# Softplus in the state-space stage: the limit on exp(-|x|) moved from VectorE to ScalarE

## The reference

```python
xz = x @ in_w
u, z = jnp.split(xz, 2, axis=-1)
uc = cb + sum((up[:, k:k + L, :] * cw[:, k] for k in range(D_CONV)))   # up: u, padded
u = jax.nn.silu(uc)
proj = u @ xpw                              # dt | Bm | Cm
delta = jax.nn.softplus(dt @ dtw + dtb)
A = -jnp.exp(A_log)
def step(h, inp):
    d_t, b_t, c_t, u_t = inp
    dA = jnp.exp(d_t[..., None] * A)
    h = dA * h + (d_t * u_t)[..., None] * b_t[:, None, :]
    return (h, jnp.einsum('bdn,bn->bd', h, c_t))
y = (ys + u * Dp) * jax.nn.silu(z)
return y @ ow                               # then x = layer_norm(y + x)
```

## Time and profile before

| | |
|---|---|
| median of 3 timed runs | 3722.86 us |
| the profiled execution | 3724.66 us |
| its span (first to last instruction) | 3722.9 us |
| mean granted TensorE clock | 0.888 of full speed |
| TensorE busy | 2960.9 us, 80% |
| VectorE busy | 2872.0 us, 77% |
| GpSimd busy | 1987.2 us, 53% |
| ScalarE busy | 1850.2 us, 50% |
| scan, 512 instructions | 1170.5 us |
| GpSimd's product with C, 512 instructions | 1212.0 us |

### The profile page before, as it was taken

The page is one execution under the profiler, slowest core; times in us unless marked ns, Lnnn a source line. Parts: engine busy times, 40 slices in busy tenths (PEclk is TensorE's granted clock), DMA queues, the critical chain, the costliest instruction groups (busy, mean ns, idle before and its releaser), DMA issues. The chain is left out here.

```text
span 3722.9 us, 48371 instructions
## 1 busy us (share of the span) xinstructions
PE 2960.9 (80%) x18386; PEld 1614.7 (43%) x18386; DVE 2872.0 (77%) x3833; ACT 1850.2 (50%) x2899; POOL 1987.2 (53%) x1022
## 2 busy tenths in 40 slices
PE   8968899556599378988898889988898889558733
PEld 3447888433477233434343434334343434234412
DVE  3667676756211349999999999999999999987688
ACT  2433343124111057766776677657775677424334
POOL 0024554212300328788888888798878887842100
PEclk8878887678699689999999999999999999888856
DMA  1000000000333323444434343444444444430000
GB/s 49 0 1 4 4 4 3 7 20 0 124 123 126 77 94 134 156 141 155 150 133 149 129 173 134 148 142 143 155 150 137 143 137 145 138 105 12 2 20 23
DMA packets 120561, 343.54 MB, mean 92 GB/s; under 512 B 14875, under 2 KB 45554, under 8 KB 119570
## 3 DMA queue, kind: packets, MB, share of 16 engines
q1 hardware_dynamic: 114450, 331.91, 26.3%
q0 software_dynamic: 3072, 6.00, 0.8%
q10 hardware_dynamic: 2816, 2.62, 0.2%
HBM read 328.21 MB, written 14.68 MB: 92 GB/s over the span
## 5 line engine op out<-in xcount | busy, mean ns | idle before, releaser
L2014 POOL TENSOR_TENSOR mb_h<-mb_h,mb_BC 128x1024 f32<-128x1024 f32 x512 | 1212.0, 2386 | 407.1 <-DVE mb_h L2261 407.1
L2261 DVE TENSOR_TENSOR_SCAN mb_h<-mb_dA,mb_bx 128x1024 f32<-128x1024 f32 x512 | 1170.5, 2286 | 23.8 <-ACT mb_dA L2128 6.0
L2364 PE MATMUL mb_y<-mb_h,ident 128*128 128x512 f32 x2048 | 998.9, 627 | 216.4 <-POOL mb_h L2014 214.3
L2128 ACT ACTIVATE mb_dA<-mb_delta,mb_A 128x511 f32<-128x511 f32 x1024 | 664.9, 713 | 417.2 <-DVE mb_h L2261 412.1
L2364 PEld LDWEIGHTS mb_y<-mb_h,ident 128*128 128x128 f32 x2048 | 386.8, 198 | 792.1 <-issue 415.9
L2257 DVE TENSOR_TENSOR mb_bx<-mb_du,mb_BC 128x1024 f32<-128x1024 f32 x512 | 630.3, 1231 | 41.4 <-DMA mb_BC<-mamba_BC 4.5
L250 PE MATMUL mb_p<-mb_xT,mb_in_w 128*128 128x512 f32 x512 | 237.3, 607 | 23.2 <-ACT mb_sz L2054 16.7
L250 PE MATMUL mb_p<-mb_upad,mb_convd 128*128 128x512 f32 x512 | 225.0, 592 | 0.8 <-ACT mb_upad L2042 0.8
L1738 DVE TENSOR_TENSOR me_h<-me_s,me_p 128x320 f32<-128x320 f32 x64 | 31.2, 488 | 220.4 <-ACT me_s L1715 220.4
L1692 POOL DMA_INDIRECT me_y<-expert_results,slot x32 | 31.1, 971 | 258.4 <-DMA expert_results<-me_oe 248.9
L250 PEld LDWEIGHTS mb_p<-mb_xT,mb_in_w 128*128 128x128 f32 x512 | 98.8, 195 | 152.3 <-issue 117.9
(11 more groups left out here) (438 smaller groups left out, 5401.3 us busy)
## 6 DMA issues: line engine op xcount, KB each, us to landing
mb_BC<-mamba_BC SPq DMA_DIRECT2D x256, 1024.0 KB, 5.2
me_W<-in_L_ffn_W SPq DMA_DIRECT2D x24, 1024.0 KB, 9.4
mb_in_w<-in_L_attn_in_proj_w SPq DMA_DIRECT2D x4, 1024.0 KB, 8.1
mb_convd<-in_mamba_taps SPq DMA_DIRECT2D x4, 1024.0 KB, 10.2
expert_rows<-me_zero SPq DMA_DIRECT2D x1, 2560.0 KB, 10.1
x<-in_x SPq DMA_DIRECT2D x4, 512.0 KB, 6.2
me_xe<-expert_rows SPq DMA_DIRECT2D x8, 256.0 KB, 10.5
expert_results<-me_oe ACTq DMA_DIRECT2D x8, 256.0 KB, 7.5
```

The costliest lines, as they stand in the source:

```text
L2014: tt(hk, hk, buffer(k, it)[:, 1, :, :], ALU.mult).then_inc(*pos(f"hc{k}{part}"))
L2128: i = av(dA[k % 2][:, c, s, 1:], delta[:, it % 2, mc, 1:], ACT.Exp, scale=A[:, MC * layer(it) + mc, n:n + 1])
L2261: nc.vector.tensor_tensor_scan(flat(h[k % NBUF][:, c, :, :]), flat(dA[k % 2][:, c, :, :]), flat(full(bx)), 0.0, ALU.mult, ALU.add).then_in ...
L2364: i = mm(ybank[c][:, :], m.ident[:, :], h[k % NBUF][:, c, s, :], start=False, stop=e == HALF - 1 and s == SU - 1)
```

## The change

The limit on e = exp(-a) is replaced by one on the exponent. With a new bias column log(S), ScalarE computes relu(a + log S) and then exp(-relu(a + log S) + log S), which is min(exp(-a), S). The first Exp now writes into lnv, not in place, so that a stays in z for it. `softplus2` is split: Exp stays at unit 9, Ln and the Relu after it (`large_log`) go to unit 10, behind the dA of unit 10; the new Relu and Exp (`small_exponential`) go to unit 11, behind the dA of unit 11 and ahead of the Silu of z columns 0 and 1. VectorE's `clip` and its semaphore go. The wait for the previous turn's delta sum moves ahead of the first Exp. In front of the loop the same pieces run one after the other.

```diff
-        shift = sb("mb_shift", [P, 4])
+        shift = sb("mb_shift", [P, 5])
...
                 def softplus2(j):
                     a.wait_ge(*acf.at("d3", j))
-                    av(z, z, ACT.Exp, scale=-1.0).then_inc(*acf("ze"))
+                    a.wait_ge(*pof.at("dl", j - 1))
+                    av(full(lnv), z, ACT.Exp, scale=-1.0).then_inc(*acf("ze"))
+
+                def large_log(j):
                     a.wait_ge(*acf.at("ze", j))
-                    a.wait_ge(*pof.at("dl", j - 1))
-                    av(full(lnv), z, ACT.Ln, bias=1.0).then_inc(*acf("ln"))
+                    av(full(lnv), full(lnv), ACT.Ln, bias=1.0).then_inc(*acf("ln"))
                     a.wait_ge(*acf.at("ln", j))
                     av(full(lnv), full(lnv), ACT.Relu, bias=shift[:, 0:1]).then_inc(*acf("mx"))
 
+                def small_exponential(j):
+                    a.wait_ge(*acf.at("ze", j))
+                    av(z, z, ACT.Relu, bias=shift[:, 4:5]).then_inc(*acf("zr"))
+                    a.wait_ge(*acf.at("zr", j))
+                    av(z, z, ACT.Exp, scale=-1.0, bias=shift[:, 4:5]).then_inc(*acf("zs"))
+
                 def softplus3(j):
-                    a.wait_ge(*dvf.at("zs", j))
+                    a.wait_ge(*acf.at("zs", j))
...
                 softplus2(0)
+                large_log(0)
+                small_exponential(0)
                 softplus3(0)
...
                             softplus2(j)
+                        if more and k == 10:
+                            large_log(j)
+                        if more and k == 11:
+                            small_exponential(j)
                         if more and k in (11, 12):
                             silu_z(j, 2 * k - 22)
                             silu_z(j, 2 * k - 21)
...
+                nc.vector.memset(shift[:, 4:5], float(np.log(SMALL)))
...
-                def clip(j):
-                    v.wait_ge(*acf.at("ln", j))
-                    tsc(z, z, SMALL, None, ALU.min).then_inc(*dvf("zs"))
...
-                clip(0)
                 first_rate()
...
-                        if more and k == 9:
-                            clip(j)
```

More of the change, by code:

```diff
@@ L1853, in mamba @@
         pps = signal("tensor_s", "D0 " + " ".join(f"y{k}" for k in us[:HALF]) + " D1 " + " ".join(f"y{k}" for k in us[HALF:]))
-        acf = signal("scalar_f", f"xT {each('u')} {each('v')} pr {each('d')} ze ln mx {each('z')}")
+        acf = signal("scalar_f", f"xT {each('u')} {each('v')} pr {each('d')} ze ln mx zr zs {each('z')}")
         acs, act_ = signal("scalar_s", per("dA")), signal("scalar_t", "res lnsqrt")
-        dvf, dvs = signal("vector_f", "zs"), signal("vector_s", per("bx", "sc"))
+        dvs = signal("vector_s", per("bx", "sc"))
         acq, acd, dvg = signal("scalar_q", "sh sq"), signal("scalar_d", "du0a du0b du1a du1b"), signal("vector_g", "gate0 gate1")
@@ L2168, in _ @@
                 flat = lambda t: t.rearrange("p s t -> p (s t)")
-                begin(v, dvf, dvs, dvg, dvt, dve2)
+                begin(v, dvs, dvg, dvt, dve2)
                 v.wait_ge(prepared, 2)
```

## The result

| | before | changed |
|---|---|---|
| median of 18 timed runs | 3722.51 us | 3735.32 us |
| profiled execution | 3724.66 us | 3735.28 us |
| its span | 3722.9 us | 3733.5 us |
| mean granted TensorE clock | 0.888 | 0.881 |

What follows compares the result with a forecast made beforehand. The second half of a turn was taken as bound by GpSimd's chain, tied with VectorE at the gate; +5.35 us (first turn) plus 15 x 0.04 us gave +5.95 us, 3728.9 us against the 3722.86 us median; range 3718 to 3740 us.

Steps and rivals of the forecast that it cites:

- the main case: Whole kernel: +5.95 us, say +6, own range 3726 to 3733 us; chance 0.70.
- the bound at the gate: Gate after unit 0: GpSimd's chain sets it, 33.67 us from its second rate step; VectorE being earlier alone gains nothing.
- the clock: Rival: z products at half clock after TensorE's new wait, 0.9 us a turn, up to +13.5 us; chance 0.17 with other late operands.
- (a): VectorE loses the limit after unit 9: 0.90 us in each of 15 turns, 13.5 us if they reach the end.
- (b): ScalarE gains Relu and Exp on the whole tile each turn, 2.00 us each; Identity ends 3.82 us later.
- (c): GpSimd's small part waits for Identity: 3.82 of 3.85 us of slack spent, price +0.04 us a turn.
- (e): First turn: Relu, table load and Exp ahead of Square have nothing to hide in, +5.35 us.
- (d): TensorE's z products of columns 2 and 3 start later but end 2.1 us before ScalarE wants them; delay absorbed.
- The sign that the prediction named against itself: Profile after: the prediction is wrong if the Silu of columns 2 and 3 waits for TensorE.
- My ground against the clock: Work behind the z products has some 3 us to spare; the clock must stay low for nearly the whole pair.
- One table for Exp and Ln: Rival: one ScalarE table serves both, saving 1.28 us loads; -9.4 us, 3713.4 us; chance 0.03.
- VectorE's time paid: Rival: GpSimd finds its operand ready, so each turn gains 0.90 us; -8.2 us, 3714.7 us; chance 0.10.

Runs made afterwards that it cites:

- c0: The changed kernel again, no edit, run beside the kernel before: 3742.78 us against 3726.59 us, ratio 1.0042.
- e3: The changed kernel with one VectorE instruction of the limit's form put back after unit 9 in each turn: 3735.95 us, ratio 1.0032 to the kernel before.
- e5: As e4, with the residual copy moved from unit 13 to unit 14: 3714.59 us, ratio 0.9969 to the kernel before.
- e6: As e5, with the first turn's limit on VectorE again: 3713.31 us, ratio 0.9964 to the kernel before.
- e2: The kernel before with VectorE's limit left out and nothing added on ScalarE (for its time alone): 3716.61 us, ratio 0.9973 to the kernel before.
- e4: As e1, with Square and Identity put ahead of the Silu of z columns 2 and 3: 3789.58 us, ratio 1.0170 to the kernel before.
- e1: The changed kernel with the new Relu and Exp put behind the Silu of z columns 0 and 1: 3730.36 us, ratio 1.0009 to the kernel before.

## Why the prediction was right, and where it was off

The measured 3735.3 us lie inside the stated range of 3718 to 3740 us, at +12.8 us where +6 was forecast. They lie outside the 3726 to 3733 us that the main case gave for itself: the direction and the bound at the gate were right, the sum was half of what came, and the range held because it had been drawn wide for the clock.

- **The bound.** The gate after unit 0 hangs on GpSimd's second rate step at a fixed distance: 33.66 to 33.71 us before, 33.7 us in c0 to e3, e5 and e6 in most halves. It is 34.2 to 35.0 us where TensorE ran its last sums at a low clock, 33.9 us in single halves of before, e2, e5 and e6, which I did not follow, and about 36.8 us in e4, where VectorE's scan waits. e3 and e2 show both sides: VectorE alone is worth nothing, VectorE with GpSimd's chain behind it 0.88 us a turn.
- **(a) VectorE's saving**, 0.90 us: measured 3.32 to 2.42 us. It lies in the gate's wait, which is 0.96 us in an undisturbed turn.
- **(b), (c) ScalarE's chain.** Forecast: Identity 3.82 us later and a price of 0.04 us a turn. Measured in undisturbed turns: 27.97 - 24.20 = 3.77 us later, 61.76 against 61.73 us, 0.03 us. The new Exp took the 2.00 us of an operation with a column.
- **(e) The first turn.** Forecast 5.35 us, measured 5.34 us up to the first scan. Of these, 0.77 us come back before the first gate, which the sum did not have.
- **(d) TensorE was the mis-sized term.** I put it at nothing, as the delayed z products had 2.1 us to spare, and kept the clock as a rival of 0.17. The wait came as reckoned (4.53 us, products starting 17.3 us after the gate), the clock fell in it, and the products took 6.67 us instead of 3.60. That is 3.07 us lost, past the 2.7 us at which I had said it decides. The sign that the prediction named against itself, a Silu of columns 2 and 3 that waits for TensorE, stands in 8 of 15 turns. So the rival was no alternative to the main case but a part of it: some 4 us in the 8 turns and 1.2 us at one gate, 6.0 us with the 0.2 us of turns 0, 12 and 13, and 8.8 us in the second profile of the same kernel. The 1.2 us at the gate need not be the change's: one half of e2 has the same.
- **The price was in the rows.** My ground against the clock was that it would have to stay low for nearly the whole pair of products. The earlier trace rows has a like case, and I did not use its length: after its wait of 4.79 us TensorE took 6.19 us for eight products of 128x512, where eight took 3.60, a loss of 2.6 us. The other turns of that trace with this wait show 5.2 to 6.8 us, losses of 1.6 to 3.2 us, on both sides of the 2.7 us that were to spare. Booked from there, the clock costs something in some of the turns, as it did.
- **Two slips.** The range up to 3740 us holds 11.1 of the clock's full 13.5 us, four fifths and not two thirds. And the gates are not VectorE's only repeated wait in the stage: the view of the earlier trace rows also has 10 waits for B and C from the DMA queues, 4.5 us; the changed kernel has 7, 4.0 us, so nothing hangs on them.
- **The rivals on the faster side.** One table for Exp and Ln: no, six loads a turn as before, and Ln has its load. VectorE's time paid: not in the changed kernel; it is in e5 and e6, where the chain is 2.5 us shorter.

The part of the clock is shown twice. In e1, with the order of two pieces swapped, the long wait and the low clock at the z products are gone, and with them 4.9 of the 6.0 us above undisturbed turns. In e3 two turns with the same wait and the same start differ in the clock alone, and only the one at 0.50 loses time. The changed kernel's own turn 3 lies between:

```profile
1819.65 5.15 PE L250 MATMUL mb_p<-mb_xT,mb_in_w 128*128 128x512 f32 x8 [4.53 <-ACT mb_sz L2054]
```

The same wait and the same place in the turn as in turn 2, but the clock is back at 1.00 earlier, the products lose 1.55 us instead of 3.07, and Identity is on time (27.97 us). So neither the wait nor the later start costs anything by itself here; how long the low clock lasts decides. What sets that length from turn to turn stays open.

## What to carry to other kernels

Before booking time taken off a busy engine, find the points where it meets the others and ask for each which engine arrived last and by how much. A meeting within 0.1 us is a tie and shows no wait in the profile; compare the instruction's start with the ends of what stands ahead of it on both engines. A saving at a tie is paid only if every arriving chain moves, so shorten or reorder the chain that feeds the other engine (here the polynomial ahead of a Silu) together with it. And where a change makes TensorE wait longer than it did, look in the trace at hand for the row behind a wait of that length, price the products behind the new wait at both clocks, and look what else stands in the queue of the engine that waits for them.

## What the runs showed of the hardware that was not expected

After waits of 4.53 us and 7.38 us TensorE ran the next products at half clock (6.67 instead of 3.60 us for eight of 128x512; 3.62 instead of 1.89 us for eight of 128x256). After a wait of about 3.6 us it did so in most turns of e3 and not in two of them, with the same instructions on both sides. The changed kernel paid 6 us and 9 us for such stretches from one profiled run to the next, partly in different turns, while its undisturbed turns all took 61.74 to 61.81 us.
